# The first chunk's routing at the end of attention A, moved up to a step sooner on VectorE and TensorE; the expert list moved behind attention

## The reference

```python
x = L0_attn_a_x                                      # (8, 512, 128)
x = x + _L0_attn_a_ref(_layernorm(x), ...)           # linear attention, elu + 1 features, rope
x = x + _L0_ffn_ref(_layernorm(x), ...)              # shared expert + the best 2 of 8 experts
x = x + _L0_attn_b_ref(_layernorm(x), ...)           # causal "log" attention
x = x + _L0_ffn_ref(_layernorm(x), ...)
# attention A, per batch and head
kv, k_sum = einsum('bhtd,bhtv->bhdv', k_feat, v), k_feat.sum(axis=2)
out = einsum('bhtd,bhdv->bhtv', q_feat, kv) / einsum('bhtd,bhd->bht', q_feat, k_sum)
# expert block, per token
probs = sigmoid(xt @ router_w.T + routing_bias)
topk_p, topk_idx = top_k(probs, 2); topk_p = topk_p / sum(topk_p)
y = shared(xt) + sum over the two of topk_p * expert(xt)
```

## Time and profile before

| | |
|---|---|
| median of 3 runs | 1031.16 us (1024.8 to 1035.87) |
| profiled execution | 1028.98 us |
| its span, first to last instruction | 1027.1 us |
| mean granted TensorE clock | 0.908 |
| TensorE busy (matmul) | 819.4 us, 80% |
| VectorE busy | 735.8 us, 72% |
| GpSimd busy | 586.9 us, 57% |
| ScalarE busy | 568.5 us, 55% |

### The profile page before, as it was taken

How to read it: one execution, slowest core, us unless ns; L and a number is a source line. 1 busy time by engine, 2 the same in 40 slices (tenths; PEclk the granted TensorE clock), 3 DMA queues, 4 the chain that set the end, 5 groups by cost and what they waited for, 6 DMA issues and landing times. The chain is left out here.

```text
span 1027.1 us, 19542 instructions
## 1 busy us (share of the span) xinstructions
PE 819.4 (80%) x6459; PEld 545.3 (53%) x6459; DVE 735.8 (72%) x1506; ACT 568.5 (55%) x805; POOL 586.9 (57%) x815
## 2 busy tenths in 40 slices
PE   3887577899986787888888888979796588899890
PEld 2666566799984333333333333333342256799890
DVE  3888745455563658899999998989789646555574
ACT  1454152133334667989898989998763242233230
POOL 2343486881383666666644444455326877788884
PEclk9999588999997878999999999999877688999996
DMA  9990012123338477584737474732210021132444
GB/s 273 300 131 1 16 39 70 54 81 114 101 84 242 124 197 220 150 227 118 234 108 215 116 208 121 224 106 55 70 42 24 32 75 39 40 102 84 132 135 122
DMA packets 114401, 124.00 MB, mean 121 GB/s; under 512 B 13328, under 2 KB 76560, under 8 KB 114176
## 3 DMA queue, kind: packets, MB, share of 16 engines
q1 hardware_dynamic: 96512, 100.80, 36.2%
q0 software_dynamic: 8416, 17.29, 5.4%
q10 hardware_dynamic: 9376, 4.65, 1.6%
HBM read 59.97 MB, written 62.72 MB: 119 GB/s over the span
## 5 line engine op out<-in xcount | busy, mean ns | idle before, releaser
L2070 DVE TENSOR_SCALAR ring_b<-psum 128x1024 int32<-128x1024 int32 x160 | 194.2, 1216 | 24.0 <-PE psum L1765 20.8
L1930 ACT ACTIVATE ring_a<-psum 128x1024 f32<-128x1024 f32 x160 | 162.4, 1021 | 51.0 <-PE psum L1765 45.7
L1936 ACT ACTIVATE ring_b<-ring_b 128x1024 f32<-128x1024 f32 x160 | 168.7, 1055 | 36.5 <-DVE ring_b L2070 36.1
L2198 POOL TENSOR_SCALAR_AFFINE_SELECT ring_b<-ring_b 128x512 f32<-128x512 f32 (+1 forms) x112 | 80.1, 728 | 171.6 <-ACT ring_b L1936 170.9
L1765 PE MATMUL psum<-stacks 32*128 32x128 f32 (+3 forms) x1024 | 98.9, 385 | 66.2 <-DVE ring_b L2070 36.8
L1765 PEld LDWEIGHTS psum<-stacks 32*128 32x128 f32 x1024 | 56.9, 193 | 173.5 <-ACT ring_a L1930 76.6
L2062 DVE TENSOR_SCALAR ring_a<-ring_a 128x1024 f32<-128x1024 f32 x160 | 119.4, 751 | 16.8 <-ACT ring_a L1930 15.0
L949 ACT ACTIVATE ring_b<-psum 128x512 f32<-128x512 f32 x72 | 42.6, 591 | 114.0 <-PE psum L834 88.0
L1818 PE MATMUL psum<-ring_b,values 128*32 128x256 f32 (+3 forms) x1024 | 94.2, 478 | 8.6 <-POOL ring_b L2198 8.6
L1797 PE MATMUL psum<-ring_a,ones_s 128*32 128x256 f32 (+3 forms) x1024 | 92.3, 469 | 9.8 <-POOL ring_a L2198 9.8
L1092 POOL DMA_INDIRECT r_rows<-y_sorted,rows_of x64 | 67.1, 1048 | 51.3 <-DMA y_sorted<-y_out 39.2
(11 more groups left out here) (220 smaller groups left out, 1484.1 us busy)
## 6 DMA issues: line engine op xcount, KB each, us to landing
stack_q<-parts SPq DMA_DIRECT2D x32, 256.0 KB
stack_ky<-parts SPq DMA_DIRECT2D x32, 256.0 KB
stacks<-stack_q SPq DMA_DIRECT2D x64, 128.0 KB
stacks<-stack_ky SPq DMA_DIRECT2D x64, 128.0 KB
stack_k<-parts SPq DMA_DIRECT2D x32, 256.0 KB
stacks<-stack_k SPq DMA_DIRECT2D x64, 128.0 KB
stack_qr<-parts SPq DMA_DIRECT2D x32, 256.0 KB
stacks<-stack_qr SPq DMA_DIRECT2D x64, 128.0 KB
```

Source lines behind the costliest of these rows:

```text
L1930: nc.scalar.activation(exps[:, n % RING, 2 * u:2 * u + 2, :], psum[:, first:first + 2, :], ACT.Exp, scale=SCALE).then_inc(self.exp, 1)
L1936: nc.scalar.activation(part, part, ACT.Ln, bias=1.0).then_inc(self.ln, 1)
L2070: nc.vector.tensor_scalar(ring[:, m % RING, HEADS_B[u][0]:HEADS_B[u][1] + 1, :].bitcast(I32), psum[:, first:first + 2, :].bitcast(I32), 0x ...
L2198: ins = nc.gpsimd.affine_select(out=part, in_=part, pattern=[[0, part.ap[1][1]], [1, 128]], compare_op=ALU.is_ge, fill=0.0, base=0, channe ...
```

## The change

Four things move; no arithmetic is added or taken away.

- VectorE: `vector_second` stands directly behind `vector_first` in step 7, ahead of the key features, the rotation and the residual sum of that step. `vector_gates` moves to the end of step 7.
- TensorE: `tensor_ranks` moves from step 8, between numerators and output, to the end of step 7, behind `a_output`.
- VectorE: `vector_pages` and `vector_rows` stand in step 8 directly behind the rotation of the keys, ahead of the division. `vector_experts` moves from the end of step 8 to the end of step 9, behind the last residual sum.
- GpSimd: the four `pool_rstd` stand behind sends 6, 10, 14 and 17 in place of 4, 8, 12 and 14.

```diff
@@ a_tensor_step
             if b > 1:
                 a_numerators(pe, b)
-            if b == 8:
-                ffn_1.tensor_ranks(pe, 0)
             if b < B:
                 a_project_q(pe, b + 1)
             if 1 <= b - AHEAD <= ffn_1.early:
                 ffn_1.turn(pe, b - AHEAD)
             if b > 1:
                 a_output(pe, b)
+            if b == 7:
+                ffn_1.tensor_ranks(pe, 0)
@@ a_vector_step
             if b <= B:
                 v.wait_ge(a_kv, b + 1)
                 a_rotate(v, b, 1, k_prod, 2, rope_k)
+            if b == 8:
+                ffn_1.vector_pages(v, 0)
+                ffn_1.vector_rows(v, 0)
             if 1 <= b - AHEAD - 1 <= ffn_1.early:
                 ffn_1.vector_logits_of(v, b - AHEAD - 1)
@@
             if b == 7:
                 ffn_1.vector_first(v, 0)
-            if b == 8:
-                ffn_1.vector_gates(v, 0)
-                ffn_1.vector_pages(v, 0)
-                ffn_1.vector_rows(v, 0)
+                ffn_1.vector_second(v, 0)
@@
             if b == 7:
-                ffn_1.vector_second(v, 0)
+                ffn_1.vector_gates(v, 0)
             if b == 8:
                 ffn_1.vector_stats(v, ffn_1.first_late)
+            if b == B + 1:
                 ffn_1.vector_experts(v, 0)
@@ attn_a_pool
-            sends = (0, 4, 8, 12, 14, 2 * ffn_1.tiles(0))
+            sends = (0, 6, 10, 14, 17, 2 * ffn_1.tiles(0))
```

## The result

The changed kernel takes 1042.23 us (median of 20 runs, 1030.49 to 1055.65), the kernel before 1029.15 us (20 runs, 1023.19 to 1037.75). The ratio is 1.0091 with a 95% interval of 1.0066 to 1.0116, so the change costs 9.4 us (1029.15 x 0.0091; 6.8 to 11.9).

The account below looks back on a forecast made before the run. Bound by a VectorE–TensorE chain ending attention A, then the bias of batch 8 waiting for GpSimd's pool_rstd. Rows 4.0 us later plus places 4.7 gave 8.7, overlapping VectorE's 7.9; on the 1031.16 median that is 1039.9 us, range 1031 to 1044.

Parts of the forecast that it names:

- Rows 4.0 us later, not sooner: Step 8, VectorE: rows_of is ready at 119.3 us instead of 115.3, with ranks and projections at the lower clock.
- This adds the wait that I think decides.: TensorE, end of step 7: ranks stand from about 98.1 to 101.9 us for the choices, with step 8's projections queued behind.
- the hold: TensorE, end of step 7: idle 3.8 us waiting for the choices, which holds back the 12 projections of step 8.
- The list: 4.6 saved at one place, nearly 4.6 lost at the next: VectorE: the list of experts leaves the path before step 9's heads, but stands before the shared expert's first product.
- VectorE's own path: VectorE after attention: first product of the shared expert 7.9 us later; VectorE reaches the bias of batch 8 at 150.0.
- the two delays: At the bias of batch 8, VectorE's path (7.9 us) and GpSimd's pool_rstd (8.7 us) overlap; only the longer counts.
- GpSimd's places, 4.7 us from the first send: GpSimd queue: the last pool_rstd stands behind 17 sends instead of 14, so 4.7 us later counted from the first send.
- One for one: Behind attention: a shift of the bias of batch 8 should reach the end of the kernel in full.
- rival 2: Shared expert: longer TensorE wait before the next logits, one more 5 us matmul stretch at lower clock; +11.2 us, chance 0.18.
- Rival 1: TensorE, steps 7 and 8: clock holds or is back during the projections; +3.6 us, 1034.8 us, chance 0.20.
- Rival 3: Faster: clock full through both steps, attention ends sooner, bias of batch 8 has slack; 1028.6 us, chance 0.06.
- Rival 4: TensorE takes projections before the ranks, which hold nothing back; rows 4.7 us sooner, total about 1031 us, chance 0.04.

Follow-up runs that it names:

- e9: Kernel before, with the second choice directly behind the first and TensorE only waiting for the choices at the end of step 7, ranks left in step 8: ratio 1.0000.
- e3: Changed kernel, with the ranks on TensorE behind the 12 projections of step 8 instead of ahead of them: ratio 1.0052 to the kernel before.
- e5: Changed kernel, with 13 extra unused matmuls on TensorE before the wait for the choices, to keep the clock up: ratio 1.0103 to the kernel before.
- e2: Kernel before, with only the list of experts moved from the end of step 8 to behind the last residual sum: ratio 1.0029.
- e4: Changed kernel, with the four pool_rstd back behind sends 4, 8, 12 and 14: ratio 1.0067 to the kernel before.
- e10: Changed kernel measured again, unaltered: ratio 1.0119 to the kernel before.
- e11: Second measurement of the kernel before with only the four pool_rstd moved behind sends 6, 10, 14 and 17: ratio 1.0036.
- e7: Kernel before, with the list of experts moved into the shared expert, behind the logits of batch 5: ratio 1.0011.
- e1: Kernel before, with only the four pool_rstd moved behind sends 6, 10, 14 and 17: ratio 1.0078.
- e6: Kernel before, with only the four pool_rstd moved earlier, behind sends 2, 7, 11 and 12: ratio 0.9992.
- e8: Kernel before, with the list of experts behind the logits of batch 5 and the four pool_rstd behind sends 2, 5, 9 and 10: ratio 0.9948.
- e12: Second measurement of the kernel before with the list behind the logits of batch 5 and pool_rstd behind sends 2, 5, 9 and 10: ratio 0.9957.

## Why the prediction was right, and where it was not

**The total and its size.** Forecast +8.7 us (ratio 1.0084), measured 1.0091 (1.0066 to 1.0116), slower and inside 1%, with the median inside the range. In the stage it holds for the reason named: the bias of batch 8 carries the shift, 8.15 us of a forecast 8.7, 3.55 from the rows and 4.6 from the places. The total fits less closely than 9.4 beside 8.7 looks: the profiled execution lost 14.8 us, the medians of all runs are 13.1 apart, and what came on top of the stage was not in the sum. That the ratio lands within 1 us of the forecast is in part luck.

**Rows 4.0 us later, not sooner.** Measured 3.55. TensorE waited 3.51 us (forecast 3.8), at the lower clock from before the ranks on; ranks and projections came as priced. Two sizes were off and nearly cancel: the clock came back in 112 to 114 us, so the sums took 1.06 us and not 2.09; and one operation of `vector_pages` (L1324) took 1.38 us and not 0.29. The remaining half us is the second choice (1.8 us and not 2.2) and the projections (4.9 us until the sums, and not 5.3).

**"This adds the wait that I think decides."** As worded, this is the step that failed. The hold alone is 1.95 us of the stage (e9), or 3.7 at equal clock, and nothing of the total. What costs is the hold together with the ranks put in front of the sums: sums start 13.73 us behind the first choice, against 10.18 with the hold alone and 5.55 before. Moving the ranks behind the projections gives 6.1 us back in the stage (e3), more than the hold: 3.9 of it is the clock (e5), 2.2 the queue. I added the hold as if nothing could absorb it, though the second choice, which stood ahead of the heads, was moved into just that gap.

**The list: 4.6 saved at one place, nearly 4.6 lost at the next.** Right: alone it moves rows to bias 8 by 0.3 us (e2). In the changed kernel the product follows it at once, at 143.04, and comes 7.5 us late (forecast 7.9).

**VectorE's own path, "7.9 us later" at the bias of batch 8.** Mis-sized: e4 shows 5.6. VectorE had also waited 1.57 us for the `pool_rstd` of batch 7, a row that I did not take into the sum. It did not move the forecast, since the longer of the two delays counted, but it is why the old places alone bring back 2.5 us and not 0.8.

**GpSimd's places, 4.7 us from the first send.** Right to 0.1 us in every kernel that has them.

**"One for one" to the end.** Not contradicted, but not exact. In the thirteen changed versions the total less the shift of the bias of batch 8 lies between -2.0 (e9) and +6.3 us (e5), 2.3 on average, with intervals of some 3 us or more on each total. Single executions differ because the stretch behind the bias took 33.5 to 38.7 us in fourteen profiles. In the changed kernel that stretch holds one at the lower clock more than in the kernel before, which was at 1.00 from 152 to 169 us. By the windows of the changed kernel:

```profile
162.00:169.00 7.00, 5.25 (x33) 4.48 (x32) 2.28 (x5) 1.98 (x4) 5.67 (x10) 0.90 0.11 37
...
171.00:177.00 6.00, 6.00 (x23) 5.42 (x24) 0.69 (x1) 1.88 (x2) 4.79 (x8) 0.50 0.12 42
```

The first row ends a stretch at the lower clock that the kernel before has as well, at 145 to 152 us; the second is the additional one. The kernel before, as far behind its bias of batch 8:

```profile
160.00:165.00 5.00, 4.68 (x29) 3.83 (x28) 1.94 (x5) 2.70 (x4) 3.95 (x7) 1.00 0.14 50
```

This sorts the last column of the table. Five profiles have such an additional stretch (changed 170 to 177 us, e10 170.5 to 174, e11 166.5 to 170, e5 168 to 171.5, e7 162 to 169), and they are the five with 36.7 us or more; the nine without it have 33.5 to 35.8. e7 has the list there as well. In the changed kernel the gate, up and down projections of the stretch take 5.9 us (171.17 to 177.09) where the same took 3.2 before (159.88 to 163.06): 2.7 of the 3.5 us behind the bias. It is also rival 2's mechanism, and the wait that the rival named grew more than it assumed, from 3.24 to 4.81 us and not by 0.8 (timeline of TensorE, changed kernel):

```profile
156.44 1.73 PE L758 MATMUL psum<-w_router,xT 128*128 128x8 f32 x8 [4.81 <-DVE ring_a L1246]
```

Whether the change makes the stretch likelier is open: both profiles of the changed kernel have it, but e11 has it and e1, the same program, has not.

**The other rivals.** Rival 1 (the clock holds): it did not hold by itself; with the filler the stage shows +4.3 us, near the rival's 3.6, but the total does not confirm it. Rival 3 falls with VectorE's wait of 2.19 us for `pool_rstd`. Rival 4 falls with the 3.51 us in front of the ranks, which no projection fills.

## What to carry to other kernels

When a step is moved sooner on an engine that must wait for its input, list what is queued behind it, and put it behind the first block that needs nothing from it: ranks behind the projections gave 6.1 us back. Where two engines deliver to one instruction (VectorE's order and GpSimd's places), moving one limit shows nothing that the total can tell (e6, e7), and moving both shows 5 us (e8). Places in a queue counted in sends are times in disguise, and each 1.57 us send must be checked against the moment when its neighbour's result is wanted.

## What the runs showed of the hardware that I had not expected

**The same program shows two times in this stage.** The kernel before, e6, e8 and e11 need 18.63 to 18.65 us to the rows, e1, e2, e7 and e12 16.88 to 16.89. e1 and e11 are one program, and so are e8 and e12. The difference of 1.75 us is the clock at the first ranks, 16 of them in 3.52 or 1.90 us. So a single profile can be off by the size of an edit, and the clock column has to be read before two stages are compared. The profile of the kernel before is of the slower kind: against one of the faster kind the changed kernel's 54.29 would be 9.9 us late at the bias of batch 8, and not 8.15 (estimate: 16.89 and 27.51 give 44.40).

**A small operation took as long as the GpSimd operation beside it.** In the changed kernel, L1324 started at 115.34 and took 1.38 us; in the kernel before the same operation took 0.29. GpSimd ran a 128x512 sum beside it (timeline of GpSimd, changed kernel):

```profile
115.31 1.26 POOL L352 TENSOR_TENSOR ring_a<-ring_a 128x512 f32<-128x512 f32 x1 [8.28 <-DVE ring_a L346]
```

It is 1.38 in both profiles of the changed kernel and in e3, e4 and e5, where pages stand directly behind the rotation that releases this sum, and 0.29 in e11, where they don't. The first operation of the gates likewise took 0.86 us in place of 0.17 beside the sum at 105.77. The Trainium skill (SBUF — State Buffer, Who interferes with whom) says that a VectorE instruction with two SBUF inputs contends with a GpSimd instruction that reads SBUF; both operations are of that kind, and the trace agrees. Moving pages ahead of the division has put 1.1 us of this onto the path.
